# First layer norm folded into the query weights and the bias pass: x loaded transposed, 512-column query products, mix and gated output from PSUM

## The reference

```python
def layernorm(x): return (x - mean(x)) / sqrt(var(x) + 1e-5)          # over channels

# cross attention, 16 heads of 32, scale = 1/sqrt(32)
Q = layernorm(x) @ W_q.T;  K = ctx @ W_k.T;  V = ctx @ W_v.T           # W_*: 512 x 512
s = Q K^T * scale - slope[head] * (query_pos - key_pos)                # -inf where mask == 0
e = exp(s - max(s));  attn = e / (1 + sum(e))
x = x + tanh(g_xattn) * (attn V) @ W_o.T

# feed forward; n = layernorm(x), n_prev = n moved by one token (0 ahead of the first)
xr = mu_r * n + (1 - mu_r) * n_prev;   xk = mu_k * n + (1 - mu_k) * n_prev
out = sigmoid(xr @ W_r.T) * (square(relu(xk @ W_k.T)) @ W_v.T)
return x + tanh(g_ffn) * out
```

## Time and profile before

| | |
|---|---|
| median of 3 runs | 1484.07 us |
| profiled execution | 1483.82 us, span 1482.0 us |
| mean granted TensorE clock | 0.991 |
| TensorE busy | 1381.9 us (93%), 10864 matmuls |
| VectorE busy | 1009.0 us (68%) |
| ScalarE busy | 887.6 us (60%) |
| GpSimd busy | 717.5 us (48%) |
| DMA | 65.96 MB, 15.2% of 16 engines |

### The profile page before, as it was taken

One profiled execution on the slowest core, in us unless ns is written; L12 is line 12 of the kernel. 1 busy time (PEld: TensorE's weight loads), 2 busy tenths in 40 slices (PEclk: granted clock), 3 DMA queues, 4 the chain that ended last, 5 costly groups with the idle time before them and its releaser, 6 DMA issues.

```text
span 1482.0 us, 33624 instructions
## 1 busy us (share of the span) xinstructions
PE 1381.9 (93%) x10864; PEld 1087.4 (73%) x10864; DVE 1009.0 (68%) x3658; ACT 887.6 (60%) x2931; POOL 717.5 (48%) x766
## 2 busy tenths in 40 slices
PE   7999899899999989999998989999999999999988
PEld 6876768677776867767686767767686777778667
DVE  5435858586685858677585868769585866858565
ACT  5247375665747466574747567474756657474652
POOL 0103555645545554655545464545556455455542
PEclk9999999999999999999999999999999999999999
DMA  8721001020100102010010202010020202001000
GB/s 267 222 76 43 15 21 60 0 64 14 57 21 28 50 0 78 0 57 21 28 50 14 64 0 57 21 46 32 16 62 0 64 14 57 21 28 50 4 27 29
DMA packets 53010, 65.96 MB, mean 45 GB/s; under 512 B 23024, under 2 KB 29168, under 8 KB 52976
## 3 DMA queue, kind: packets, MB, share of 16 engines
q1 hardware_dynamic: 52976, 65.52, 15.2%
HBM read 40.87 MB, written 24.64 MB: 44 GB/s over the span
## 4 chain that ended last, share of the span: by engine, by line
PE 43%; DVE 17%; issue 15%; POOL 9%; ACT 9%; DMA 5%; SPq 0%; DVEq 0%; POOLq 0%; ACTq 0%
PE rotating L401 27%; PE probs_bank L561 8%; ACT probs L775 5%; PE attn_bank L575 4%; POOL square L1368 4%; DVE diff L1109 3%; POOL xnt_or_act L1370 3%; DVE relu L1109 3%; DMA xs<-in_x_dram 2%; DVE square L1104 2%; PE score_bank L401 2%; DVE norm L1026 2%; POOL probs L1331 1%; DVE mix_k L1104 1%; POOL mixed_key L1358 1%
## 5 line engine op out<-in xcount | busy, mean ns | idle before, releaser
L775 ACT ACTIVATE probs<-probs,neg_max 128x120 f32<-128x120 f32 x1024 | 391.0, 386 | 19.6 <-DVE neg_max L1048 19.6
L1331 POOL TENSOR_TENSOR probs<-probs,recip 128x960 f32<-128x960 f32 x128 | 229.4, 1792 | 259.9 <-DVE recip L1062 259.9
L401 PE MATMUL rotating<-mixed_key,w_key 128*128 128x512 f32 x720 | 197.7, 414 | 36.5 <-ACT gated L827 36.5
L401 PE MATMUL rotating<-w_proj,attn_t 128*128 128x512 f32 x768 | 209.8, 413 | 20.6 <-ACT gated L827 18.6
L783 ACT COPY probs_t<-probs_bank 120x512 f32<-120x512 f32 x256 | 149.9, 585 | 116.8 <-PE probs_bank L561 116.4
L1048 DVE CUSTOM_DVE_ANT_0 probs<-score_bank,mask_in 128x120 f32<-128x120 f32 x1024 | 215.0, 275 | 4.3
L401 PE MATMUL rotating<-w_value,xnt_or_act 128*128 128x512 f32 x720 | 203.4, 411 | 5.5 <-POOL xnt_or_act L1370 5.3
L401 PE MATMUL rotating<-xnt_or_act,w_query 128*128 128x256 f32 x1536 | 198.7, 286 | 0.5 <-DVE xnt_or_act L1032 0.5
L775 ACT ACTIVATION_READ_ACCUMULATOR probs<-probs,neg_max 128x1 f32 x1024 | 194.7, 190 | 0.0
L401 PE MATMUL rotating<-w_gate,mixed_gate 128*128 128x512 f32 x768 | 189.7, 399 | 0.0
L401 PEld LDWEIGHTS rotating<-xnt_or_act,w_query 128*128 128x128 f32 x1536 | 187.8, 191 | 1.9 <-DVE xnt_or_act L1032 0.8
(11 more groups left out here) (126 smaller groups left out, 2162.6 us busy)
## 6 DMA issues: line engine op xcount, KB each, us to landing
xs<-in_x_dram SPq DMA_DIRECT2D x64, 256.0 KB, 3.0
out_dram<-gated SPq DMA_DIRECT2D x64, 256.0 KB, 3.0
value_scratch<-gated SPq DMA_DIRECT2D x16, 240.0 KB, 2.9
mask_in<-in_mask_dram SPq DMA_DIRECT2D x16, 240.0 KB, 2.7
keys_t<-key_scratch SPq DMA_DIRECT2D x16, 240.0 KB, 3.4
values<-value_scratch SPq DMA_DIRECT2D x16, 240.0 KB, 3.7
probs<-in_ctx_t_dram SPq DMA_DIRECT2D x6, 480.0 KB, 7.2
key_scratch<-query_t SPq DMA_DIRECT2D x12, 240.0 KB, 5.0
```

The lines of the kernel that those rows point to most:

```text
L401: mm = pe.matmul(bank, stationary(a, c), moving(b, c), start=(i == 0), stop=(i == MATMULS - 1))
L775: e = act.activation(probs[:, t % 2, head, :], probs[:, t % 2, head, :], ACT.Exp, bias=neg_max[:, t % 2, head:head + 1], scale=-1.0, accum ...
L1331: pool.tensor_tensor(part, part, recip[:, t % 2, heads].unsqueeze(2).to_broadcast((P, H // 2, NK)), ALU.mult)\
```

## The change

The layer norm ahead of the queries is folded away. W_q is centred on the chip (the mean over its input channels is taken off), so the product needs no mean of x. 1/std of a token goes into the bias pass: the distance is multiplied by std, and the pass multiplies by minus slope times 1/std, read from a tile. So the queries are made from x itself, which the host hands in a second time, transposed in tiles (`x_t`).

- `normalise1`, `turn1`, `turn1_out`, `turn1_low` go. `load_xt` (SP, 256 KB a tile, two slots `x_turned`; tiles 0 and 1 of the next batch at the start of a round in `turned_ahead`, tiles 2 and 3 ahead of the mask load), `xt_split` (ScalarE, high part) and `xt_rest` (GpSimd, low part) come. `rstd1_of` makes 1/std and std and, as a third operation, the 16 scales of the tile.
- A query product is 12 matmuls of 512 columns, one product to a bank instead of two halves; it waits for all four tiles of x.
- `difference` (GpSimd) goes; `mix` subtracts on VectorE, in place in the PSUM bank of turn2, and its products read that bank. The bank is free only after the mix.
- `finish` writes its first result into the PSUM bank of the value product and reads it from there; the bank is free only after its second operation.
- turn2 0 moves behind gate 3 and into score bank 0; the rotation of the two banks shifts with it (proj 1, value 2, gate 3, proj 2 change places). On GpSimd, `edge` 0 and 1 stand later in the order.
- In the load stage the mean of W_q is made by four fp32 matmuls on TensorE behind the first chunk, taken off by VectorE, and ScalarE's copy of W_q waits for it.

```diff
 ATTENTION_AND_FFN = (
...
-    ("proj", 0, 0), ("value", 0, -1), ("value", 1, -1), ("gate", 2, -1), ("turn2", 0, 0), ("proj", 1, 0),
-    ("value", 2, -1), ("gate", 3, -1), ("proj", 2, 0), ("turn1", 1, 1),
+    ("proj", 0, 0), ("value", 0, -1), ("value", 1, -1), ("gate", 2, -1), ("proj", 1, 0),
+    ("value", 2, -1), ("gate", 3, -1), ("proj", 2, 0),
-SPARE_BANKS = {("turn1", 0): "score_bank0", ("turn2", 1): "score_bank1", ("turn1", 2): "probs_bank",
-               ("turn2", 2): "attn_bank", ("turn1", 3): "attn_bank", ("turn2", 3): "probs_bank"}
+SPARE_BANKS = {("turn2", 0): "score_bank0", ("turn2", 1): "score_bank1", ("turn2", 2): "attn_bank",
+               ("turn2", 3): "probs_bank"}
 # SP
             load_mask(0)
+            for t in range(2):
+                load_xt(0, t)
...
+            for t in range(2, QT):
+                sp.wait_ge(xt_low, t - 1)
+                load_xt(0, t)
...
+            def turned_ahead(b):
+                for t in range(2):
+                    sp.wait_ge(xt_low, b * QT + t + 3)
+                    load_xt(b + 1, t)
...
                     if t == 1 and not last:
+                        for n in range(2, QT):
+                            sp.wait_ge(xt_low, (b + 1) * QT + n - 1)
+                            load_xt(b + 1, n)
                         sp.wait_ge(scores_biased, (b + 1) * QT * G)
                         load_mask(b + 1)
 # TensorE
             chunk(0, 0, True)
+            pe.wait_ge(averaging_ready, 1)
+            pe.wait_ge(raw_weight[0], 32)
+            for c in range(CT):
+                mm = pe.matmul(probs_bank[:], averaging, xs[:, 0, c, :], start=(c == 0), stop=(c == CT - 1))
+            mm.then_inc(wq_mean_done, 1)
             chunk(0, 1, False)
...
-                        pe.wait_ge(read[what], (b + rel + back) * 4 + n + 1)
+                        freed = {"value": out_ready, "turn2": mixg_ready}.get(what, read[what])
+                        pe.wait_ge(freed, (b + rel + back) * 4 + n + 1)
...
+            def query(b, m, steps):
+                if steps[0] == 0:
+                    pe.wait_ge(xt_low, (b + 1) * QT)
+                return product(bank_of["query", m][:], lambda s, c: w_query[:, s, c, m * P:(m + 1) * P],
+                               lambda s, c: xt_or_act[:, s, c, :], steps)
...
                 use("gate", 2)
-                use("turn2", 0)
                 use("proj", 1)
                 with_attention(2, "value", 2)
                 use("gate", 3)
-                use("turn1", 0)
+                use("turn2", 0)
                 use("turn2", 1)
                 with_attention(3, "proj", 2)
-                use("turn1", 1)
                 use("value", 3)
                 use("proj", 3)
-                use("turn1", 2)
+                use("turn2", 2)
                 use("query", 0)
...
-                use("turn2", 2)
-                use("query", 1, range(7))
-                use("turn1", 3)
-                use("query", 1, range(7, MATMULS))
+                use("query", 1)
                 use("turn2", 3)
 # ScalarE
             def weight(i):
                 act.wait_ge(raw_weight[i % 2], 16 * (i // 2 + 1))
+                if raw[i] is wq:
+                    act.wait_ge(wq_centred, 1)
                 act.copy(split[i][:, HI], xs[:, i % 2]).then_inc(weight_high, 1)
...
+            def xt_split(b, t):
+                act.wait_ge(xt_loaded[t % 2], b * 32 + (t // 2 + 1) * 16)
...
+                act.copy(xt_or_act[:, HI, :, t * P:(t + 1) * P], x_turned[:, t % 2]).then_inc(xt_high, 1)
...
                 feed_forward((gate_out, 2))
-                turn2_out(b, 0)
+                if ffn:
+                    after((xt_split, 0), (xt_split, 1))
                 exps(b, 3, 0)
...
                 feed_forward((gate_out, 3))
+                if not ffn:
+                    after((xt_split, 0), (xt_split, 1))
+                after((xt_split, 2))
+                turn2_out(b, 0)
                 probs_out(b, 3, 0)
-                after((turn1_out, 0))
+                turn2_out(b, 1)
                 probs_out(b, 3, 1)
-                turn2_out(b, 1)
                 probs_out(b, 3, 2)
                 mix_key_high(b, 0)
                 probs_out(b, 3, 3)
...
-                after((turn1_out, 1), (turn1_out, 2), (query_out, 0))
+                after((xt_split, 3))
                 turn2_out(b, 2)
 # VectorE
+            dve.wait_ge(wq_mean_done, 1)
+            dve.tensor_tensor(xs[:, 0], xs[:, 0], probs_bank[:].unsqueeze(1).to_broadcast((P, CT, D)), ALU.subtract)\
+                .then_inc(wq_centred, 1)
             weight(2)
...
+                    dve.wait_ge(scale1_ready, b * QT + t + 1)
-                                                 in1=neg_dist[:, t, :], scale=-SLOPES[head], scalar=BIG,
+                                                 in1=neg_dist[:, t, :], scale=score_scale[:, t, head:head + 1], scalar=BIG,
...
             def mix(b, t):
-                dve.wait_ge(diff_ready, b * QT + t + 1)
+                turned = bank_of["turn2", t][:].rearrange("p (c q) -> p c q", c=CT)
+                previous = xn2t[:, t % 2, :, 0:P]
+                dve.wait_ge(xn2t_ready, b * QT + t + 1)
+                dve.wait_ge(edge_ready, b * QT + t + 1)
+                dve.tensor_tensor(turned, turned, previous, ALU.subtract).then_inc(diff_ready, 1)
...
             def finish(b, t, banks=bank_of):
-                dve.scalar_tensor_tensor(out=gated[:, t % 2], in0=gated[:, t % 2], scalar=1.0, in1=banks["value", t][:],
-                                         op0=ALU.add, op1=ALU.mult).then_inc(read["value"], 1)
+                dve.scalar_tensor_tensor(out=banks["value", t][:], in0=gated[:, t % 2], scalar=1.0, in1=banks["value", t][:],
+                                         op0=ALU.add, op1=ALU.mult).then_inc(value_gated, 1)
...
+                dve.wait_ge(rstd1_ready, (b + 1) * QT)
+                dve.tensor_tensor(neg_dist, neg_dist, rstd1[:, :, 1:2].to_broadcast((P, QT, NK)), ALU.mult)\
+                    .then_inc(dist_ready, 1)
 # GpSimd
             def rstd1_of(b, t):
...
+                pool.tensor_scalar(score_scale[:, t, :], neg_slopes[:], rstd1[:, t, 0:1], None, ALU.mult)\
+                    .then_inc(scale1_ready, 1)
+            def xt_rest(b, t):
+                pool.wait_ge(xt_high, b * QT + t + 1)
+                part = xt_or_act[:, :, :, t * P:(t + 1) * P]
+                pool.tensor_tensor(part[:, LO], x_turned[:, t % 2], as_f32(part[:, HI]), ALU.subtract).then_inc(xt_low, 1)
...
                 normalise_probs(b, 2, 1)
-                edge(b, 0)
-                difference(b, 0)
+                if ffn:
+                    after((xt_rest, 0), (xt_rest, 1))
                 rstd2_of(b, 1)
                 normalise_probs(b, 3, 0)
                 normalise_probs(b, 3, 1)
                 after((rstd1_of, 1))
+                if not ffn:
+                    after((xt_rest, 0), (xt_rest, 1))
+                after((xt_rest, 2))
+                edge(b, 0)
+                after((rstd1_of, 2))
                 edge(b, 1)
-                difference(b, 1)
-                after((rstd1_of, 2))
+                rstd2_of(b, 2)
                 mix_low(b, 0)
-                rstd2_of(b, 2)
+                after((xt_rest, 3), (rstd1_of, 3))
                 if last:
                     mix_low(b, 1)
-                after((rstd1_of, 3))
                 rstd2_of(b, 3)
```

More of the change, by code:

```diff
@@ L547, in late_product @@
                 return mm
[L549 removed]
+            made = {"key": key, "gate": gate, "value": value, "proj": proj, "turn2": turn2,
                     "query": query}
@@ L587, in use @@
                     if (what, tile) in SPARE_BANKS:
[L588 to L591 removed]
+                        free_spare(b, (what, tile))
+                        made[what](b, tile, steps).then_inc(done[what], 1)
                         return
@@ L660, in _ @@
             pe.wait_ge(ident_ready, 1)
-            first = [u for u in ATTENTION_AND_FFN if u[0] in ("turn1", "query")]
-            for t in range(QT):
-                turn1(0, t, None).then_inc(done["turn1"], 1)
+            first = [u for u in ATTENTION_AND_FFN if u[0] == "query"]
             for u in range(4):
```

212 lines of the change are left out of this document (91 added, 121 removed).

## The result

The changed kernel takes **1512.09 us** (median of 4 runs, 1509.45 to 1514.47) against 1484.35 for the kernel before on the same chip: ratio 1.0187, 95% interval 1.0169 to 1.0206. It is slower by about 28 us; the forecast was 1489. The granted clock is 0.973 against 0.991; TensorE is busy as long as before with 1016 matmuls fewer.

The account below looks back on a forecast made before the run. Within a round, VectorE's chain was taken to bound the stretch to the end of tile 1's attention, though TensorE is 93% busy. 19 + 5 - 15 x 2.9 + 14 x 1.6 - 1.5 + 4 = +5.4: 1489 us, range 1475 to 1503.

Parts of the forecast that it names:

- Clock: Behind the new wait on TensorE in the rounds, slow clock of 1.4 us in 0.2 of 14 rounds: +4 us.
- slow clock after every new wait: Rival: the clock falls behind the new wait in the other 80% of rounds too, 1505 us; chance 0.14.
- A to B: Round from end of tile 1's attention (A) to end of tile 3's (B): wait of 2.45, +1.6 us a round.
- B to A: Round from end of tile 3's attention (B) to end of tile 1's (A): VectorE's chain shorter, -2.9 us a round.
- Load stage: Before the first queries: W_q's mean and centring and the x_t loads delay chunks and queries, +19 us (10 to 22).
- the other rule of the Trainium skill that I weighed: VectorE instructions with two SBUF inputs block against GpSimd reading SBUF: std multiply costs 1.3, gain 2.6 instead of 2.9.
- Batch 0: First batch: x copies and tile 2's load delay TensorE, +7.5 less some 2.2, so +5 us (-2 to 9).
- tail: Last round: no next x queued before edge 0, so proj 1's -1.1 stays: -1.5 us (-3 to 0).
- Edge in time: Rival: GpSimd reaches edge 0 before TensorE wants tile 3's third probability transpose, 1451 us; chance 0.17.
- The pointer's rival: Rival: the bias pass with its pointer scale, not ScalarE, sets the exponentials, +1 us a round, 1503; chance 0.09.
- Every sign that I had named: No 2.46 before first key product; wait near 2.4 before third transpose; mixes 3.05; gap about 5 after mean; first query about 102.
- the two that were to prove the forecast wrong: A round under 83 us, or a first query before 92.

Follow-up runs that it names:

- Experiments 2 and 3: Changed kernel with edge 0 only ahead of xt_rest 2: 1475.74 us; changed kernel with six idle matmuls ahead of tile 3's third transpose: 1491.92 us.
- experiment 5: Kernel with edge 0 early (1457.88 us), plus VectorE's distances, except the multiply by std, moved ahead of normalise2 3: 1441.81 us.
- experiment 4: Changed kernel with the mix's difference written to SBUF instead of back into the PSUM bank: 1521.03 us.
- experiment 1: Changed kernel with GpSimd's edge 0 moved early, ahead of normalise_probs(2,0): 1457.88 us.
- experiment 6: Changed kernel with the bias pass scaled by constant minus slope instead of a value read from a tile: 1506.04 us.
- 7a: Changed kernel with the mean of W_q between key and value products of the first chunk: 1504.64 us.
- 7c: Changed kernel with a place for each x_t tile of batch 0, all loaded behind the last context loads: 1505.92 us.
- 7b: Changed kernel without the mean of W_q, its subtraction and the wait of ScalarE's copy: 1501.82 us.

## Why the prediction was wrong

- **The term that failed is *Clock*: "14 x 0.2 x 1.4 = +4".** The 1.4 was right (1.3 measured); the 0.2 was wrong: the clock fell behind the new wait in 14 of 14 rounds, +18. I took the share from another place, where 4 of 15 rounds fell after a wait of the same length. Experiments 2 and 3 show the clock as a cost of its own. My rival "slow clock after every new wait" was the true case, with a chance of 0.14.
- The share was also read from one execution, and an unusual one. Its four rounds are the last four in a row; this is the first of them, and the eleven before took 3.01 to 3.06:

```profile
1121.22 4.38 PE L401 MATMUL rotating<-mixed_key,w_key 128*128 128x512 f32 x12 [2.46 <-ACT gated L827]
```

  Its granted clock was 0.991, while the 27 other executions of the kernel before that ran beside the experiments have 0.978 to 0.988 and take about as long (1482 to 1488 us). Eleven more such falls, at 1.4 us of 1482 each, would bring 0.991 to about 0.98: an estimate by which the clock fell there in nearly every round of most executions, though no trace shows it.
- *A to B*, +1.6 a round: the row of releasers and the wait (2.46 for 2.45) were right. 0.3 more a round, +4 to 5 in all, is the start: GpSimd's row behind the reciprocals began at A + 17.6 instead of 17.4, and rstd1_of took 1.6 instead of 1.27, since its power of two columns takes 0.72, of one 0.57, and the third operation starts 0.26 behind it. With the slow clock (4.59 from the third transpose to B for 3.4) that makes the 3.1.
- *B to A*, -2.9: right, and experiment 5 shows that VectorE's row sets it. That the bias pass came at B + 24.9 to the tenth is luck: mix 1 started 0.25 late, the three mixes took 0.5 less than forecast and distances 0.2 more. The mix in PSUM gives about 1.4 (experiment 4, whose theory had 2 to 3.9); the earlier start of mix 1, at B + 12.2 for 13.7, is 1.5.
- *Load stage*, +19: right as a sum (19.2) from parts that offset each other, so in part by luck. The last chunk ends 13.2 late, not 14.5, of which the centring's row is 9.0 to 11.5, not 12.6; the wait of the first queries grew by 4.2, not 4.8; and their slow clock, 1.8, was not in it.
- The mean of W_q took 3.60, not 2.8. My estimate by the Trainium skill (FP8 and Floating Point Precision, TensorE Precision Notes: true fp32 is four passes) was 4.0: the trace is nearer to the rule than to the value I took. The multiply by std took 0.66, and GpSimd stood still beside it, so the changed kernel does not test the other rule of the Trainium skill that I weighed (SBUF — State Buffer, Who interferes with whom). Experiment 5 does: beside GpSimd's subtract the same multiply took 1.59, as by that rule.
- *Batch 0* and *tail*: 4.2 with one B to A, forecast 0.6; the wait of 8.78 is the one named, for which I had 9.35 - 1.4 = 7.95, put down as 7.5.
- "Edge in time" would have been 1451; experiment 1, which makes it so, gives 1458. The pointer's rival is refuted by experiment 6. Every sign that I had named came (no wait before the first key product, 2.46 before the third transpose, the first query near 102), and none of the two that were to prove the forecast wrong: they tested the waits and not the clock behind them.

## What to carry to other kernels

Moving a tiny instruction (a 0.11 us memset) behind three steps of 1.3 to 1.8 us on a half-idle engine cost 54 us here, because a copy on another engine stands behind its reader: list, for each moved instruction, what it is queued behind and who waits for it, and if its true dependency is old, issue it early. Price a new wait on TensorE in a repeated round twice, with and without the slow clock behind it, as all rounds or none; a share read from one execution at another place was no guide, so look at the granted clock of several executions first. When a sum comes out right, look at its parts: the load stage gave 14 us back to two changes of order and place (7a and 7c) although its total had been forecast.

## What the runs showed of the hardware

- At one place of the round, a wait of 2.46 was followed by the 1.2 GHz level in 14 of 14 rounds of the changed kernel, of 7a and of 7c, in 13 of experiment 6 and 12 of 7b; 1.24 in 0 of 14, and 0.9 behind six filling matmuls in 0 of 14. But in experiment 4 the same 2.46 was followed by it in 6 of 14, and before in 4 of 15 elsewhere: length alone doesn't decide, and what does stays open.
- VectorE products with one operand in PSUM took 1.12 to 1.13 a group beside GpSimd and alone; with both in SBUF, 1.12 to 2.45 (before: up to 3.90). The multiply of two operands in SBUF took 0.66 alone and 1.59 beside GpSimd's subtract (experiment 5).
- A scale read from SBUF instead of a constant costs 60 ns an operation of 120 columns in the bias pass (277 to 337, experiment 6).
